# An attention and expert kernel on one core: the attention phase written anew, with every turning done by transposing DMAs

## The chip, the cores and the metric

One core of one Trainium2 chip runs the whole kernel. The metric is the device time of one execution in microseconds (us); lower is better. Below, PE is TensorE, PEld its weight loads, DVE is VectorE, ACT is ScalarE, POOL is GpSimd and SP is SyncE, whose queue issues the DMAs that no other engine issues. PSUM is the memory of eight banks (128 partitions x 2 KB each) into which PE writes.

## The reference

32 batches of 128 tokens with 512 numbers each pass through one attention layer and one mixture-of-experts layer:

```python
x = x + xattn(layernorm(x), mask, ctx)          # 32 heads of 16 numbers
x = x + moe(layernorm(x))                       # 8 experts, the best 2 for each token

def xattn(h, mask, ctx):
    q, k, v = h @ Wq, h @ Wk, h @ Wv            # split into 32 heads
    q, k = rope(q), rope(k)
    w = softmax(q @ k.T / 4 + mask)             # over the batch's own 128 keys
    out = w @ v
    a_k, a_v = ctx @ Wk, ctx @ Wv               # 128 more keys, no rope, no mask
    out += tanh(gate) * softmax(q @ a_k.T / 4) @ a_v
    return out @ Wo

def moe(h):                                     # 2 of 8 experts by router logits
    gate, up = split(h @ w1[e]); y = (silu(gate) * up) @ w2[e]
```

There are thus two softmaxes for each head and batch: the "own" path (path 0, masked) and the "adapter" path (path 1).

## The kernel before

The kernel has two phases, each a block in which every engine has its own program; engines meet only at semaphores. The attention phase goes through the 32 batches and writes the residual sum, the normalized rows for the experts (`h_pairs`) and eight lists of tokens. The expert phase then works through 71 tiles of 128 listed rows; it isn't touched by the change.

Matmuls of f32 accuracy are made of f16 halves: a value is split into a high part and what is left (`xcs`, `ohs`, `qs`, `ks`, `aks` hold both), and `project` sums three terms of four chunks each, 12 matmuls of 512 columns. There are six large projections for each batch: `q`, `k`, `ak`, `v`, `avp`, `out_project`.

PE contracts over partitions, so what it contracts must be turned. Before the change PE turns it, by matmuls with an identity, and ACT copies the result out of PSUM:
- `x_turn`, `out_turn`, `h_turn` (helper `transposes`, L1075): 8 tiles of 128x128 each for the normalized input, the attention's output and the normalized rows of the router, and three ACT copies (`x_turned`, `out_T`, `h_transposed`; L530, L598, L609).
- `stack` (helper `turn_pairs`, L1120): q, k and adapter k of two heads at a time, 48 tiles for each batch, into the banks `ma`, and eight ACT copies `stack_out` (L570) into `qkk`. `qkk` is a ring of five slots; a slot holds one octet of heads (8 heads: 4 pairs of 2 rows of 64 partitions).

The scores are computed twice. First directly, queries on the partitions, to get each query's maximum: `half_scores` (L1145) writes 4 heads of one path to one of the two banks `md`, DVE adds the mask (L795, path 0 only) and takes the maxima (`maxima`, L799, one call a bank). PE turns the maxima (`max_turn`, L1156). Then turned, keys on the partitions, which the product with the values wants: `scores_T` writes to the two banks `st` first the turned mask as two f32 matmuls of 512 columns for each bank (L1172), then adds the scores (L1178) and the negative maxima (L1183). ACT takes the exponential bank by bank (`exps`, L576), PE multiplies with the values (`values`, L1197) into the banks `av`, and the sums go back through ACT (`values_T`, L582) and PE (`values_back`, L1205).

Every engine's order is written out by hand. The function `step(b, c, d, n, m)` of each engine is called once a batch: b is the batch whose turned scores are under way, n the next, m the one after it, d and c the two before. Each engine works strictly in the order of its `step`, so a wait holds back all that stands behind it. The code outside the loop, `first` and `last`, fills and empties this order.

SP issues seven plain loads and stores in a batch's step, among them `wst` (a slice of the expert weights, which ACT and POOL split while attention runs).

## Time and profile before

| | |
|---|---|
| time, median of 3 runs | 1954.81 us (1952.67 to 1966.75) |
| profiled execution, span | 1957.9 us |
| PE busy | 1802.3 us, 92% |
| DVE busy | 1245.6 us, 64% |
| ACT busy | 1075.1 us, 55% |
| POOL busy | 751.8 us, 38% |
| DMA queue of SP | 65.96 MB, 10.3% of 16 engines' span |

The span runs from the first to the last instruction of one profiled execution. An engine is busy while an instruction runs on it; matmuls overlap one another, so their durations add up to more than the time that PE takes for them, and the time of a kind is better read from start to start. The page also shows the span in 40 slices, with the busy share of each engine in tenths.

### The profile page before, as it was taken

What the parts mean: (1) busy time and instruction counts of PE and PEld (TensorE: products, weight loads), DVE (VectorE), ACT (ScalarE), POOL (GpSimd) and SP (SyncE); (2) the same over time, 40 slices, a digit from 0 to 9 for tenths busy, and PEclk for the clock granted to TensorE, in tenths of its full rate; (3) what the DMA queues carried; (4) which work ended last, traced back from release to release, by engine and by line L of the source; (5) the groups of instructions that cost most, each with busy time, mean ns of one, the idle gap of its engine ahead of it and who ended that gap; (6) DMA issues with size and microseconds to landing.
All of it is one profiled execution on the core that took longest, in us unless ns stands there. A gap on an engine that the chain in (4) does not pass through costs nothing. (4 is left out here: it accounts for less than half of the span.)

```text
span 1957.9 us, 53291 instructions
## 1 busy us (share of the span) xinstructions
PE 1802.3 (92%) x19721; PEld 1094.1 (56%) x19722; DVE 1245.6 (64%) x3365; ACT 1075.1 (55%) x1716; POOL 751.8 (38%) x926
## 2 busy tenths in 40 slices
PE   3899899999999999999999999999845999999997
PEld 1555455555555555555555556555523666666664
DVE  4578677777788877778887777888644323332332
ACT  3465556666666666666666666666524444344432
POOL 3233433433333334433333443333223444444443
PEclk8899999999999999999999999999977999999999
DMA  3011111111111111111111111110014444444443
GB/s 135 26 37 37 37 38 37 38 43 43 62 38 38 37 37 43 44 62 38 38 37 38 43 50 55 38 38 32 29 63 112 82 85 85 80 82 86 84 79 63
DMA packets 64021, 106.00 MB, mean 54 GB/s; under 512 B 19088, under 2 KB 23184, under 8 KB 63312
## 3 DMA queue, kind: packets, MB, share of 16 engines
q0 software_dynamic: 18144, 37.31, 10.8%
q1 hardware_dynamic: 45680, 65.96, 10.3%
q8 instruction: 137, 2.24, 0.5%
q14 instruction: 60, 0.49, 0.1%
HBM read 67.51 MB, written 35.72 MB: 53 GB/s over the span
## 5 line engine op out<-in xcount | busy, mean ns | idle before, releaser
L576 ACT ACTIVATE pr<-st 128x512 f32<-128x512 f32 x512 | 285.5, 601 | 267.2 <-PE st L1183 248.3
L799 DVE TENSOR_REDUCE mx<-md 128x4 f32<-128x512 f32 x512 | 340.7, 688 | 20.8 <-PE md L1145 7.2
L1566 PE MATMUL y<-w1s,hgT 128*128 x1704 | 279.9, 315 | 3.6 <-ACT hgT L1480 3.6
L570 ACT ACTIVATE qkk<-ma 128x768 f16<-128x768 f16 x256 | 205.8, 817 | 84.2 <-PE ma L1120 84.2
L450 POOL TENSOR_TENSOR part<-part,tg_r 128x128 f32<-128x128 f32 x128 | 51.4, 402 | 474.8 <-DVE part L832 474.8
L1566 PEld LDWEIGHTS y<-w1s,hgT 128*128 128x128 f16 x1704 | 164.3, 98 | 95.5 <-issue 4.0
L1145 PE MATMUL md<-qkk 64*128 64x128 f16 x2048 | 166.8, 219 | 48.1 <-DVE mx L799 42.5
L795 DVE TENSOR_TENSOR md<-md,msk 128x512 f32<-128x512 f32 x256 | 177.1, 692 | 50.4 <-PE md L1145 50.4
L1197 PE MATMUL av<-pr,vv 128*17 128x128 f32 x4096 | 176.6, 277 | 2.8 <-ACT pr L576 2.1
L1145 PEld LDWEIGHTS md<-qkk 64*128 64x128 f16 x2048 | 100.6, 94 | 111.8 <-issue 85.6
L1480 ACT ACTIVATE hgT<-px 128x1024 f16<-128x1024 f16 x71 | 72.6, 1023 | 156.6 <-PE px L1556 156.6
L1172 PE MATMUL st<-identr,mskp 128*128 128x512 f32 x512 | 156.1, 426 | 1.3 <-DVE mT L822 0.8
L1585 PE MATMUL y<-w2s,yT 128*128 (+1 forms) x639 | 150.3, 379 | 0.9 <-DVE yT L1544 0.9
L1543 DVE COPY yT<-py 128x256 f16<-128x256 f16 x142 | 40.3, 284 | 148.2 <-PE py L1575 148.2
L760 DVE SCALAR_TENSOR_TENSOR aks<-ma,aks 128x512 f16<-128x512 f32 x64 | 41.2, 686 | 126.0 <-ACT aks L536 126.0
L1459 POOL DMA_INDIRECT out<-yo,dst x71 | 113.1, 1593 | 16.7 <-issue 12.1
L1197 PEld LDWEIGHTS av<-pr,vv 128*17 128x17 f32 x4096 | 81.4, 96 | 63.9 <-issue 32.7
L582 ACT ACTIVATE avT<-av 128x512 f32<-128x512 f32 x128 | 77.4, 604 | 56.8 <-PE av L1197 56.8
L407 POOL TENSOR_TENSOR t<-t 128x512 f32<-128x512 f32 x32 | 50.4, 1576 | 148.3 <-DVE t L773 148.3
L1172 PEld LDWEIGHTS st<-identr,mskp 128*128 128x128 f32 x512 | 88.8, 188 | 33.1 <-issue 6.9
L1178 PE MATMUL st<-qkk 64*128 64x128 f16 x2048 | 101.8, 219 | 0.2
L1183 PE MATMUL st<-mT,hsel 64*128 64x128 bf16 x2048 | 99.1, 216 | 0.0
(206 smaller groups left out, 3578.3 us busy)
## 6 DMA issues: line engine op xcount, KB each, us to landing
wst<-in_w SPq DMA_DIRECT2D x32, 352.0 KB, 3.1
cin<-in_ctx SPq DMA_DIRECT2D x32, 256.0 KB, 3.9
xin<-in_x SPq DMA_DIRECT2D x32, 256.0 KB, 3.5
xres<-in_x SPq DMA_DIRECT2D x32, 256.0 KB, 3.9
out<-x SPq DMA_DIRECT2D x32, 256.0 KB, 2.1
h_pairs<-ohs SPq DMA_DIRECT2D x32, 256.0 KB, 2.0
msk<-in_mask SPq DMA_DIRECT2D x32, 64.0 KB, 3.6
lrow<-lists SPq DMA_DIRECT2D x71, 1.0 KB, 3.5
```

The costliest lines, as they stand in the source:

```text
L570: act.activation(qkk[:, slot, :, j:j + 2, :], turned, ACT.Copy).then_inc(stk_o.sem, 1)
L576: act.activation(pr[:, r, :, :], st[r][:, :, :], ACT.Exp).then_inc(p_ex.sem, 1)
L795: dve.tensor_tensor(sm[r][:, :, :], sm[r][:, :, :], msk[:, n.par, :].unsqueeze(1).to_broadcast([P, 4, P]), ALU.add).then_inc(s_mask.sem, 1)
L799: dve.tensor_reduce(mx[:, 2 * path + r, 4 * o:4 * o + 4], sm[r][:, :, :], AX.X, ALU.max).then_inc(s_max[r].sem, 1)
L1145: i = pe.matmul(sm[r][:, j, :], qkk[rows, slot, 0, j, :], qkk[rows, slot, 1 + path, j, :], start=True, stop=True)
L1172: pe.matmul(st[r][:, :, :], mskp[:, n.par, part, :], identr[:, :].unsqueeze(1).to_broadcast([P, 4, P]), start=(part == 0), stop=False, ski ...
L1178: pe.matmul(st[r][:, j, :], qkk[rows, slot, 1 + path, j, :], qkk[rows, slot, 0, j, :], start=(path == 1 and j == 0), stop=False, skip_grou ...
L1183: i = pe.matmul(st[r][:, j, :], hsel[rows, p:p + 1].to_broadcast([64, P]), mT[rows, path, :], start=False, stop=(j == 3), skip_group_check ...
L1197: i = pe.matmul(av[o % 2][VC * j:VC * j + VW, 2 * path + r, :], vv[:, n.par, path, 8 * o + 2 * j + r, :], pr[:, r, j, :], start=True, stop ...
L1459: pool.indirect_dma_start(out=dram["out_rows"], out_offset=bass.IndirectOffsetOnAxis(ap=dst[:, s.off % LB:s.off % LB + 1], axis=0), in_=yo ...
L1566: i = pe.matmul(y1[s.par][j][:, 0:F], hgT[:, s.par, a, c, :], w, start=(n == 0), stop=(n == 11))
L1585: i = pe.matmul(y2[s.par][:, :], yT[0:fn, a, k, :], w, start=(n == 0), stop=(n == 8))
```

## The change

The expert phase stays. In the attention phase:
- All turning but that of the maxima and of the values' sums moves to transposing DMAs of SP: three of 128x1024 f16 (256 KB) for x, output and router rows, and twelve of 128x512 f16 (128 KB) for q, k and adapter k by octet, in each batch. `x_turn`, `out_turn`, `h_turn`, `stack` and the ACT copies behind them go.
- The mask comes twice, plain and turned (`mask_T`, turned on the host). ACT writes it into the banks before the scores are added: `seed_direct` into both banks `md`, `seed_turned` into both banks `st`, 1024 columns each, once an octet. The mask matmuls of PE (L1172) and the mask additions of DVE (L795) go, and so do the splits of the mask (L546, L712).
- The two banks `st` become one tensor, and so do the two `md`. `exps` and `maxima` take both banks with one instruction (1024 columns). `direct` alternates between the two halves of partitions, so that two small matmuls of different rows stand side by side.
- `ctx_lo` and `out_low` move from DVE to POOL.
- `xres` has one buffer and not two; the normalized rows have their own tile `hn`; `mT` gets a second buffer.
- Every engine gets a new order. `step(i)` runs each task for batch i minus a constant of its own; there is no `first` or `last`. `latest` puts one wait before a PE task that takes a bank which other groups have used. SP's order holds 15 transposing and 8 plain DMAs in each step.

The diff, cut to its core:

```diff
-    st = [ps(f"st{k}", [P, 4, P], F32) for k in range(2)]
+    st = ps("st", [P, 2, 4, P], F32)
     ma = [ps(f"ma{k}", [P, 512], F32) for k in range(2)]
-    md = [ps(f"md{k}", [P, 512], F32) for k in range(2)]
+    md = ps("md", [P, 2, 4, P], F32)
+    home = dict(q=1, k=0, ak=0, v=1, avp=0, o=1, router=0, places=1, mturn=1)
...
     @block.sync
+        def turn_x(n):
+            sp.wait_ge(x_lo.sem, x_lo.at(n))
+            for used in (q_p, k_p, v_p):
+                sp.wait_ge(used.sem, used.at(n.shift(-1)))
+            sp.dma_start_transpose(turned(xT), rows(xcs)).then_inc(x_T.sem, 16)
...
+        def turn_octet(n, o, plane, src, split, done):
+            slot, past, octet = place_of(n, o)
+            sp.wait_ge(split.sem, split.at(n))
+            sp.wait_ge(t_pe.sem, t_pe.at(past, 4 * octet + 4))
+            sp.dma_start_transpose(qkk[:, slot, plane, :, :],
+                                   src[:, 8 * o:8 * o + 8, :, :].rearrange("p h a d -> p (h a d)")
+                                   ).then_inc(done[o].sem, 16)
...
+        def step(i):
+            run(turn_q, i - 13, 2)
+            run(turn_k, i - 13, 2)
+            run(turn_ak, i - 13, 2)
+            run(turn_out, i - 15)
+            run(next_m_turned, i - 13)
+            run(next_w, i - 14)
+            run(turn_k, i - 13, 3)
+            run(load_residual, i - 15)
+            run(next_m, i - 12)
+            run(turn_q, i - 13, 3)
+            run(turn_ak, i - 13, 3)
+            run(store_out, i - 16)
+            run(turn_q, i - 12, 0)
+            run(next_x, i - 10)
+            run(turn_k, i - 12, 0)
+            run(turn_ak, i - 12, 0)
+            run(turn_q, i - 12, 1)
+            run(turn_x, i - 11)
+            run(next_c, i - 11)
+            run(turn_k, i - 12, 1)
+            run(turn_h, i - 15)
+            run(turn_ak, i - 12, 1)
+            run(store_h, i - 15)
...
     @block.scalar
-            act.activation(mskp[:, n.par, 0, :], msk[:, n.par, :], ACT.Copy).then_inc(m_hi.sem, 1)
+        def seed_direct(n, o):
+            act.wait_ge(d_max.sem, d_max.at(n, 2 * o))
+            act.activation(md[:, :, :, :].rearrange("p r j n -> p (r j) n"),
+                           msk[:, n.par, :].unsqueeze(1).to_broadcast([P, 8, P]), ACT.Copy).then_inc(d_seed.sem, 1)
+        def seed_turned(n, o):
+            act.wait_ge(p_ex.sem, p_ex.at(n, 2 * o))
+            act.activation(st[:, :, :, :].rearrange("p r j n -> p (r j) n"),
+                           mskT[:, n.par, :].unsqueeze(1).to_broadcast([P, 8, P]), ACT.Copy).then_inc(t_seed.sem, 1)
-        def stack_out(n, g):
-            act.activation(qkk[:, slot, :, j:j + 2, :], turned, ACT.Copy).then_inc(stk_o.sem, 1)
-        def exps(n, u):
-            r = u % 2
-            act.wait_ge(t_pe.sem, t_pe.at(n, u + 1))
-            act.wait_ge(av_pe.sem, av_pe.at(n, u - 1))
-            act.activation(pr[:, r, :, :], st[r][:, :, :], ACT.Exp).then_inc(p_ex.sem, 1)
+        def exps(n, w):
+            act.wait_ge(t_pe.sem, t_pe.at(n, 2 * w + 2))
+            act.wait_ge(av_pe.sem, av_pe.at(n, w))
+            act.activation(pr[:, :, :, :], st[:, :, :, :], ACT.Exp).then_inc(p_ex.sem, 1)
...
     @block.vector
-                if path == 0:
-                    dve.tensor_tensor(sm[r][:, :, :], sm[r][:, :, :],
-                                      msk[:, n.par, :].unsqueeze(1).to_broadcast([P, 4, P]),
-                                      ALU.add).then_inc(s_mask.sem, 1)
-                dve.tensor_reduce(mx[:, 2 * path + r, 4 * o:4 * o + 4], sm[r][:, :, :], AX.X,
-                                  ALU.max).then_inc(s_max[r].sem, 1)
+        def maxima(n, o, path):
+            dve.wait_ge(d_pe.sem, d_pe.at(n, 2 * (2 * o + path) + 2))
+            dve.tensor_reduce(mx[:, 2 * path:2 * path + 2, 4 * o:4 * o + 4], md[:, :, :, :], AX.X,
+                              ALU.max).then_inc(d_max.sem, 1)
...
     @block.tensor
+        def direct(n, o, path):
+            if path == 0:
+                pe.wait_ge(d_seed.sem, d_seed.at(n, o + 1))
+                pe.wait_ge(q_T[o].sem, q_T[o].at(n))
+                pe.wait_ge(k_T[o].sem, k_T[o].at(n))
+            else:
+                pe.wait_ge(d_max.sem, d_max.at(n, 2 * o + 1))
+                pe.wait_ge(ak_T[o].sem, ak_T[o].at(n))
             for j in range(4):
-                i = pe.matmul(sm[r][:, j, :], qkk[rows, slot, 0, j, :], qkk[rows, slot, 1 + path, j, :],
-                              start=True, stop=True)
-            i.then_inc(s_pe[r].sem, 1)
+                for r in range(2):
+                    rows = slice(64 * r, 64 * r + 64)
+                    i = pe.matmul(md[:, r, j, :], qkk[rows, slot, 0, j, :], qkk[rows, slot, 1 + path, j, :],
+                                  start=(path == 1 and j == 0), stop=(j == 3), skip_group_check=True)
+                    if j == 3:
+                        i.then_inc(d_pe.sem, 1)
...
-            if path == 0:
-                for r in range(2):
-                    for part in range(2):
-                        pe.matmul(st[r][:, :, :], mskp[:, n.par, part, :],
-                                  identr[:, :].unsqueeze(1).to_broadcast([P, 4, P]), start=(part == 0), stop=False,
-                                  skip_group_check=True)
```

## Rows read from the trace of the kernel before

**Rows 1.** The page: busy time, and the busy tenths in 40 slices.
```profile
PE 1802.3 (92%) x19721; PEld 1094.1 (56%) x19722; DVE 1245.6 (64%) x3365; ACT 1075.1 (55%) x1716; POOL 751.8 (38%) x926
...
PE   3899899999999999999999999999845999999997
```

**Rows 2.** Windows to the first L1156, to the last, to the first gather, the rest.
```profile
core 0: us, PE busy (x) PEld busy (x) DVE busy (x) ACT busy (x) POOL busy (x), PEclk, DMA share, GB/s
0.00:69.40 69.40, 36.53 (x199) 18.87 (x201) 35.32 (x60) 24.86 (x30) 14.70 (x35) 0.80 0.26 96
69.40:1408.10 1338.70, 1284.60 (x15810) 773.32 (x15809) 1030.39 (x2606) 835.72 (x1352) 505.69 (x586) 0.99 0.13 41
1408.10:1479.00 70.90, 28.84 (x377) 16.50 (x375) 35.29 (x123) 25.63 (x42) 16.33 (x23) 0.73 0.21 67
1479.00:1957.90 478.90, 452.31 (x3337) 285.45 (x3337) 144.61 (x577) 188.87 (x293) 215.08 (x283) 0.97 0.47 83
```

**Rows 3.** The window of one batch, from one turning of the maxima to the next.
```profile
722.33:765.02 42.69, 41.33 (x514) 24.98 (x514) 33.57 (x87) 27.18 (x44) 16.32 (x19) 1.00 0.13 43
```

**Rows 4.** Groups of that batch, PE (busy, mean ns, idle before, releaser).
```profile
L1145 PE MATMUL md<-qkk 64*128 64x128 f16 x64 | 5.1, 217 | 1.4 <-DVE mx L799 1.2
```

**Rows 5.** Timeline of PE within that batch (start, length, line, operation).
```profile
736.85 1.21 PE L1172 MATMUL st<-identr,mskp 128*128 128x512 f32 x4
737.99 0.40 PE L1178 MATMUL st<-qkk 64*128 64x128 f16 x8
738.22 0.39 PE L1183 MATMUL st<-mT,hsel 64*128 64x128 bf16 x8
738.57 0.28 PE L1120 MATMUL ma<-ident,qs 128*128 128x128 f16 x2
...
739.25 0.61 PE L1205 MATMUL av<-identr,avT 128*128 128x128 f32 x4
...
744.65 0.43 PE L1145 MATMUL md<-qkk 64*128 64x128 f16 x8
...
761.17 0.83 PE L1145 MATMUL md<-qkk 64*128 64x128 f16 x8
```

**Rows 6.** Groups of that batch, DVE.
```profile
L799 DVE TENSOR_REDUCE mx<-md 128x4 f32<-128x512 f32 x16 | 10.6, 688 | 0.6 <-PE md L1145 0.2
L795 DVE TENSOR_TENSOR md<-md,msk 128x512 f32<-128x512 f32 x8 | 5.5, 693 | 1.4 <-PE md L1145 1.4
L832 DVE TENSOR_TENSOR part<-av,rc 128x256 f32<-128x256 f32 x4 | 1.7, 424 | 0.1
```

**Rows 7.** Groups of that batch, ACT.
```profile
L576 ACT ACTIVATE pr<-st 128x512 f32<-128x512 f32 x16 | 8.9, 602 | 8.2 <-PE st L1183 7.9 <-PE av L1197 0.3
L570 ACT ACTIVATE qkk<-ma 128x768 f16<-128x768 f16 x8 | 6.4, 818 | 2.4 <-PE ma L1120 2.4
...
L551 ACT ACTIVATE qs<-t 128x1024 f16<-128x1024 f32 x1 | 1.0, 1048 | 0.0
L536 ACT ACTIVATE aks<-ma 128x1024 f16<-128x1024 f32 x1 | 1.0, 1024 | 0.0
```

**Rows 8.** Groups of that batch, POOL.
```profile
L402 POOL TENSOR_TENSOR xcs<-nat,xcs 128x512 f16<-128x512 f32 x1 | 1.2, 1156 | 3.8 <-ACT xcs L509 3.8
```

**Rows 9.** Timeline of SP's queue in that batch: a DMA's issue.
```profile
741.02 0.33 SPq L315 DMA_DIRECT2D h_pairs<-ohs  x1
...
745.85 0.43 SPq L285 DMA_DIRECT2D xin<-in_x  x1
```

**Rows 10.** The page: SP's DMA queue, and DMA issues with us to landing.
```profile
q1 hardware_dynamic: 45680, 65.96, 10.3%
...
wst<-in_w SPq DMA_DIRECT2D x32, 352.0 KB, 3.1
cin<-in_ctx SPq DMA_DIRECT2D x32, 256.0 KB, 3.9
...
h_pairs<-ohs SPq DMA_DIRECT2D x32, 256.0 KB, 2.0
```

More of the change, by code:

```diff
@@ L244, in whole, with run, walk, latest @@
         return isinstance(n.n, int) and n.n == 0
-    def walk(eng, step, first, last):
-        def near(b, lacks):
-            step(b, *(None if d in lacks else b.shift(d) for d in (-2, -1, 1, 2)))
-        first(Batch(0, 0))
-        for n in range(NB):
-            b = Batch(0, n)
-            near(b, [d for d in (-2, -1, 1, 2) if not 0 <= n + d < NB])
-        last(Batch(0, NB - 1))
+    def run(task, n, *args):
+        if 0 <= n < NB:
+            task(Batch(0, n), *args)
+    def walk(step):
+        for i in range(NB + 16):
+            step(i)
+    def latest(eng, n, *users):
+        for event, shift in users:
+            if 0 <= n.n + shift < NB:
+                eng.wait_ge(event.sem, event.at(n.shift(shift)))
+                return
     def place_of(n, o):
@@ new lines, in turn_q, with turn_k, turn_ak, load_first_w2 @@
+        def turn_q(n, o):
+            turn_octet(n, o, 0, qs, q_lo, q_T)
+        def turn_k(n, o):
+            turn_octet(n, o, 1, ks, k_lo, k_T)
+        def turn_ak(n, o):
+            turn_octet(n, o, 2, aks, ak_lo, ak_T)
+        def load_first_w2(n):
+            for used in (q_p, k_p, ak_p, v_p, av_p):
+                sp.wait_ge(used.sem, used.at(n))
+            for e in range(len(keep["w2f"])):
+                sp.dma_start(keep["w2f"][e][:, 0:2, :], dram["w2a"][e]).then_inc(keep["w2_in"][e], 16)
+                sp.dma_start(keep["w2f"][e][0:96, 2, :], dram["w2b"][e]).then_inc(keep["w2_in"][e], 16)
@@ L554, in k_high @@
             act.wait_ge(k_r.sem, k_r.at(n))
[L555 removed]
+            for turned in k_T:
+                act.wait_ge(turned.sem, turned.at(n.shift(-1)))
             act.activation(ks[:, :, 0:4:2, :], twice(t3), ACT.Copy).then_inc(k_hi.sem, 1)
@@ L1065, in experts_slots, with step @@
             assert made[0] == TAB
-        walk(dve, step, first, last)
+        def step(i):
+            run(residual, i - 5)
+            run(maxima, i - 3, 3, 1)
+            run(neg_max, i - 3)
+            run(turned_max, i - 3)
+            run(stats_h, i - 5)
+            run(ak_low, i - 2)
+            run(norm_h, i - 5)
+            run(normal, i - 4, 2)
+            run(h_low, i - 5)
+            run(maxima, i - 2, 0, 0)
+            run(stats_x, i)
+            run(normal, i - 4, 3)
+            run(router_weights, i - 6)
+            run(maxima, i - 2, 0, 1)
+            run(router_counts, i - 6)
+            run(normal, i - 3, 0)
+            run(maxima, i - 2, 1, 0)
+            run(norm_x, i)
+            run(rotate_q, i - 1)
+            run(maxima, i - 2, 1, 1)
+            run(router_rows, i - 6)
+            run(rotate_k, i - 1)
+            run(maxima, i - 2, 2, 0)
+            run(normal, i - 3, 1)
+            run(router_logits, i - 5)
+            run(maxima, i - 2, 2, 1)
+            run(router_top, i - 5)
+            run(maxima, i - 2, 3, 0)
+        walk(step)
+        experts_slots()
     @block.tensor
     def _(pe):
-        def transposes(bank, src):
-            for part in range(2):
-                for c in range(NC_):
-                    i = pe.transpose(half(bank)[:, part * NC_ + c, :], src[:, part, c * P:(c + 1) * P], ident16[:, :])
-            return i
         def project(bank, xt, w, cols=D):
@@ new lines, in _, with step @@
+        pe.wait_ge(dve_c.sem, 2)
+        for bank in (st[:, 0, :, :], st[:, 1, :, :], md[:, 0, :, :], md[:, 1, :, :]):
+            i = pe.matmul(bank, ident_bf[:, :], ident_bf[:, :].unsqueeze(1).to_broadcast([P, 4, P]),
+                          start=True, stop=True)
+        i.then_inc(banks_open.sem, 1)
+        def step(i):
+            run(scores_T, i - 6, 4)
+            run(k, i - 4)
+            run(scores_T, i - 6, 5)
+            run(values, i - 6, 4)
+            run(direct, i - 5, 2, 0)
+            run(values_back, i - 6, 1)
+            run(router, i - 8)
+            run(values, i - 6, 5)
+            run(direct, i - 5, 2, 1)
+            run(scores_T, i - 6, 6)
+            run(out_project, i - 7)
+            run(direct, i - 5, 3, 0)
+            run(scores_T, i - 6, 7)
+            run(values, i - 6, 6)
+            run(values_back, i - 6, 2)
+            run(direct, i - 5, 3, 1)
+            run(ak, i - 4)
+            run(max_turn, i - 5)
+            run(values, i - 6, 7)
+            run(scores_T, i - 5, 0)
+            run(v, i - 4)
+            run(values_back, i - 6, 3)
+            run(scores_T, i - 5, 1)
+            run(direct, i - 4, 0, 0)
+            run(values, i - 5, 0)
+            run(avp, i - 4)
+            run(values, i - 5, 1)
+            run(direct, i - 4, 0, 1)
+            run(scores_T, i - 5, 2)
+            run(places, i - 8)
+            run(values_back, i - 5, 0)
+            run(values, i - 5, 2)
+            run(scores_T, i - 5, 3)
+            run(direct, i - 4, 1, 0)
+            run(q, i - 3)
+            run(values, i - 5, 3)
+            run(direct, i - 4, 1, 1)
```

805 lines of the change are left out of this document (266 added, 539 removed).

## The prediction

> **What bounds the kernel now.** I read the page first, for the shares by engine and by slice. PE is busy for 92% of the span and in nearly every slice of the first 28, while DVE, ACT and POOL are busy for 64%, 55% and 38% [rows 1]. The windows then cut the span in four [rows 2]: 69.4 us until the first batch's maxima are turned, 1338.7 us from there to the same instruction of the last batch, 70.9 us of emptying up to the first gather, and 478.9 us of experts. The second stretch holds 31 steps of one batch, so a step takes 1338.7 / 31 = 43.18 us. That number is what the change can move; the experts aren't touched. In one step of 42.69 us PE is busy for 41.33, DVE for 33.57, ACT for 27.18 and POOL for 16.32 [rows 3]. PE sets the step: it stands still for some 1.4 us only, nearly all of it before L1145, waiting until DVE has read the banks `md` [rows 4]. So each us of PE work taken out of a step is worth 31 us, until another engine, a chain through the banks, or SP's queue takes over.
>
> **The change part by part, PE first.** Durations of matmuls overlap, so I take starts.
> - Mask matmuls: four from 736.85 to 737.99, 1.14 us, and four such groups a batch: 4.6 us go [rows 5].
> - Turning q, k and adapter k: twelve tiles from 738.57 to 739.25, 0.68 us or 57 ns each; 48 tiles are 2.7 us, with the gaps to the next work about 2.9 us. The 24 tiles of `transposes` at the same 57 ns are 1.4 us. Together 4.3 us go [rows 5].
> - Direct scores: the eleven merged rows of L1145 in this batch (first and last in [rows 5]), each counted from its start to the start of the next row, come to 5.9 us for 64 matmuls, stalls included. Side by side they become what the turned scores are already: eight of L1178 from 737.99 to 738.22, 0.23 us [rows 5]. 64 of those take 1.9 us, so 4.0 us go if the stalls go with them. The stalls are DVE's, and DVE becomes faster (below).
> - Values, projections, the negative maxima and the sums' way back stay as they are.
>
> PE's work in a step is then 42.7 - 4.6 - 4.3 - 4.0 = 29.8 us. This is the floor of the step, a gain of 13.4 us on 43.18.
>
> **DVE.** The mask additions go, 5.5 us [rows 6]. Sixteen reductions of 512 columns at 0.688 us become eight of 1024. No row has that form; 256 columns take 0.424 and 512 take 0.69 us, which is 1.04 ns a column [rows 6], so 1024 take about 1.22 us, and 11.0 becomes 9.8 us. `ctx_lo` and `out_low`, of 512 columns too, leave with some 0.7 us each, and the mask split with a quarter of that size, 0.3 us. DVE has 33.6 - 5.5 - 1.2 - 1.7 = 25.2 us of work.
>
> **ACT.** Eight copies to `qkk` at 0.818, three of 1024 columns at 1.02 and the mask's high part at 0.3 go: 9.9 us. Sixteen exponentials at 0.602 (9.6 us) become eight of 1024 columns; the nearest rows of that size are 1.02 from PSUM and 1.05 from SBUF [rows 7], so 8.2 us. Eight seeds at 1.05 come, 8.4 us; no row writes 1024 f32 columns to PSUM, and I take the reading rows for both ends. ACT has 27.2 - 9.9 - 1.4 + 8.4 = 24.3 us. The seeding thus costs ACT nearly what the copies give back, and it is free only because ACT isn't the bound: were it the bound, it would cost 8.4 x 31 = 260 us.
>
> **POOL** takes two subtractions of 512 columns, 1.16 us each [rows 8]: 16.3 + 2.3 = 18.6 us.
>
> **The chains through the banks.** A bank pair is now used as a whole and has no second copy. For `st` an octet runs: seed 1.05, scores and negative maxima about 0.6, exponential 1.02, scores 0.6, exponential 1.02; 4.3 us, with five hand-overs of some 0.1 to 0.15 us about 4.9, four octets 20 us. For `md`: seed 1.05, then twice scores of about 0.4 and a reduction of 1.22, again 4.9 and 20 us. Both are under 29.8. The ring of five slots closes a third chain: octet 3 of the next batch can be turned only once octet 2 of this one has been used in `scores_T`; its direct scores, maxima, the turning of the maxima (with DVE's five small steps, an estimated 2.5 us) and two thirds of the next `st` chain (15 us) stand behind that. With three transposing DMAs of 3 to 4 us from issue to landing I get 24 to 26 us a step. So the chains are 4 to 10 us shorter than the floor of PE, which must cover all queueing behind other tasks. In the kernel before, the same kind of hand-written order loses 1.4 of 42.7 us.
>
> **SP's queue, the unknown.** Fifteen transposing DMAs come in each step; no row of this trace is one. Behind each stand, in order, the other turnings and all loads, and behind these PE. What the rows say: a plain issue holds the queue for 0.33 to 0.43 us [rows 9], so eight plain ones are 3.0 us, and fifteen more at 0.4 would be 6. That is the lower bound, 9 us of a step. From issue to landing a plain 256 KB takes 2.0 us as a store and up to 3.9 us as a load [rows 10]. If each transposing DMA held the queue until it landed, a step would be 15x + 3.0 us with x between 2.0 and 3.9: 33 to 61.5 us, the upper bound. In bandwidth, 12 x 128 KB + 3 x 256 KB is 2.4 MB; the queue's present 65.96 MB took 10.3% of 1957.9 us, 327 GB/s [rows 10], at which they are 7 us on the sixteen engines. I take a holding time under 1.8 us, where the queue isn't the bound (15 x 1.79 + 3.0 = 29.8), since the nearest rows in kind, the issues of the same queue, are a quarter of that; the landing rows stay as the upper end.
>
> On this the Trainium skill speaks both ways, and no row here can decide. "Advanced Engine Details and Errata", section "X-Bar Transpose (TRN2)", has transposing DMAs as fast as plain ones. Against the change speaks a table in "DMA: Bandwidth & Descriptors", section "Why a DMA increments its semaphore by 16 and not by 1": on generations before the newest, the issuing engine spends 262,144 cycles on 8,192 tiles turned from SBUF to SBUF, 32 cycles a tile. It names no tile size; if a tile were 2 KB, 128 KB would hold SP for 2,048 cycles, and at the 1.2 GHz of "TensorE: Matmul & The Clock Gate" a step would be an estimated 18 x 1.7 + 3.0 = 34 us.
>
> **The sum.** To the 29.8 us I add 1.5 us for waits that remain (the kernel before has 1.4) and 0.5 us because the mean step before (43.18) was that much longer than the one that I took apart. The step is 31.8 us, and the 31 steps give 31 x (43.18 - 31.8) = 353 us. Filling and emptying, 69.4 and 70.9 us, stay about as they are: PE has slack there, and each turning on the way of the first and the last batch trades an ACT copy of 1 us behind PE for a DMA of 2 to 4 us; I add 5 us. 1957.9 - 353 + 5 = 1610 us. The median of the runs lies 3 us under the profiled execution, so 1607 us.
>
> **The rivals.**
> 1. The chains, not PE. The `md` and `st` chains share ACT, whose work is 24 of 30 us, and DVE, with 25 of 30; a seed that is late behind another ACT task delays scores, maxima and the ring. For it: no bank has a partner any more, and each loop needs three engines. Against: 4 to 10 us of slack. It gives steps of 34 to 37 us, taking 35.5: 1957.9 - 31 x 7.7 + 5 - 3 = 1721 us. In the trace ACT and DVE would wait for each other around `md` and `st`, with PE under 90%.
> 2. SP's queue is the bound, but below the old step. A holding time between 1.8 and 2.68 us (15x + 3.0 between 30 and 43.2) does it; near 2.3 us the step is 37.5 us, 1957.9 - 31 x 5.7 + 5 - 3 = 1783 us. For it: 23 issues in order, each with waits of its own, and the store's landing of 2.0 us [rows 10] falls in this band. Against: plain issues don't hold the queue until they land. The skill's rule of 32 cycles a tile belongs here, and with a tile of 2 KB it ends near 1670 us.
> 3. The other side: the same mechanism with the price of a load. Once a transposing DMA keeps the queue for more than 2.68 us, the step passes 43.2 us and the kernel is slower. At the 3.1 us of the fastest load row [rows 10] the step is 49.5 us and the time 1957.9 + 31 x 6.3 + 5 - 3 = 2155 us. PE would then stand still for many us at a stretch, and its clock, 0.99 of full in the steady stretch and 0.73 to 0.80 where PE waits a lot [rows 2], would fall too.
> 4. That the floor is lower than I think (the direct scores cost nothing beside others, or the waits vanish): 29.5 us and no waits is 1957.9 - 31 x 13.7 = 1533 us, the low end.
>
> **How the numbers follow.** A measurement of this kernel can tell about 1% from no change, 20 us. The forecast (PE bound, steps of 30 to 33.5 us, 1550 to 1660 us) has 0.58, with what lies under it. Rival 1 has 0.13, rival 2 has 0.15, rival 3 has 0.12, and 0.02 is left for a time near the old one. All but rival 3 and that rest are faster: 0.86 faster, 0.02 the same, 0.12 slower. The range goes from 1535, the floor, to 1800, which takes in rival 1 and most of rival 2 and leaves rival 3 and the rest of rival 2 out.
>
> **What would show it.** In the new profile: a PE step of 30 to 33 us between two turnings of the maxima; PE busy over 90% in it; eight reductions near 1.22 us and sixteen ACT instructions near 1.0 us for seeds and exponentials; DVE about 25, ACT about 24 and POOL about 19 us a step. SP's issues of transposing DMAs in the timeline show the holding time at once: under 1.8 us I am right on the queue, above it rivals 2 and 3 follow with their sums. What makes me wrong most is that holding time, then waits of PE for `q_T`, `k_T`, `d_seed` or `t_seed`.

## The result, and the profile after

The changed kernel takes 1854.84 us, the median of 4 runs (1844.53 to 1861.64), beside 1956.3 us for the kernel before on the same chip: 0.9452 of its time, 95% interval 0.9405 to 0.95. It is 5.5% faster. The prediction said 1607 us and 18%, and its range ended at 1800. The profiled execution has a span of 1842.8 us. Its page, with the busy shares, PE's tenths and granted clock in 40 slices, SP's DMA queue and the largest groups, answers to [rows 1, 6, 7, 10]:

```profile
PE 1506.1 (82%) x16909; PEld 864.2 (47%) x16910; DVE 1111.3 (60%) x2755; ACT 1023.0 (56%) x1332; POOL 835.0 (45%) x991
...
PE   4788777888888787788878888887519999999996
...
PEclk9999899998999999989999899999659999999999
...
q1 hardware_dynamic: 360560, 143.61, 40.6%
...
L787 DVE TENSOR_REDUCE mx<-md 128x8 f32<-128x1024 f32 x256 | 313.0, 1222 | 238.4 <-PE md L1071 235.4
L646 ACT ACTIVATE pr<-st 128x1024 f32<-128x1024 f32 x256 | 260.9, 1019 | 167.8 <-PE av L1116 135.6
...
L623 ACT ACTIVATE st<-mskT 128x1024 f32<-128x1024 f32 x128 | 131.8, 1030 | 5.6
```

PE lost 296 us of work, as planned, but its slices in the attention phase read 7 and 8 where they read 9 [rows 1]. No engine is full any more. The windows cut where [rows 2] cut say how much is idle:

```profile
0.00:68.00 68.00, 32.12 (x164) 12.79 (x165) 37.62 (x51) 22.89 (x25) 30.16 (x44) 0.90 0.47 132
68.00:1286.50 1218.50, 993.86 (x13060) 549.52 (x13064) 887.77 (x1987) 786.54 (x981) 563.30 (x631) 0.95 0.57 104
1286.50:1364.00 77.50, 27.12 (x360) 16.06 (x348) 40.93 (x143) 24.67 (x34) 27.27 (x36) 0.60 0.36 105
```

The 31 steps take 1218.5 us, 39.3 us each, where 31.8 was forecast. PE is busy for 993.9 / 31 = 32.1 us of a step (29.8 forecast) and idle for 7.2 us (1.5 forecast, and 0.5 for the mean step). DVE is busy for 28.6 us of a step, where 25.2 was forecast; ACT (25.4) and POOL (18.2) lie within 1.1 us of their forecasts. Everything outside these steps takes 624.3 us, 5.1 us more than before; the forecast added 5 for it. So the whole miss lies in the step. The view of waits for the same stretch (total us, times, longest) names what PE waits for, and what holds ACT:

```profile
ACT ohs L663 <- DMA h_pairs<-ohs: 96.1, 29, 4.4
...
PE av L1116 <- ACT pr L646: 71.9, 62, 3.3
...
PE ma L1080 <- DVE mp L805: 53.4, 27, 2.8
PE md L1071 <- DMA qkk<-qs: 44.0, 19, 3.7
...
PE md L1071 <- issue: 27.2, 12, 4.8
...
PE md L1071 <- DMA qkk<-ks: 14.3, 18, 1.7
```

Four things hold PE, none for more than 72 us: the exponentials (2.3 us a step), the split maxima `mp` (1.7), the turned q and k of an octet (1.9), and 0.9 for which the profile names no releaser. How they come about is seen in one step, from one turning of the maxima (705.37) to the next (746.06). First SP's queue, in the timeline (start, length; the length is the time that the DMA holds the queue):

```profile
730.29 1.20 SPq L347 DMA_TRANSPOSE qkk<-ks  x1
731.53 0.58 SPq L288 DMA_DIRECT2D xres<-in_x  x1
732.15 2.43 SPq L298 DMA_DIRECT2D msk<-in_mask  x1
734.68 1.20 SPq L347 DMA_TRANSPOSE qkk<-qs  x1
```

This step is the slowest of its kind: 2.43 us is the longest that the mask's load holds the queue, and its median over the stretch is 0.43 us. An ordinary step has k and q 2.4 us apart and not 4.4:

```profile
528.48 1.20 SPq L347 DMA_TRANSPOSE qkk<-ks  x1
...
530.34 0.43 SPq L298 DMA_DIRECT2D msk<-in_mask  x1
530.87 1.80 SPq L347 DMA_TRANSPOSE qkk<-qs  x1
```

Then PE, its timeline in the first of these steps (in brackets: idle before, and the releaser):

```profile
723.67 0.63 PE L1116 MATMUL av<-pr,vv 128*17 128x128 f32 x16 [2.62 <-ACT pr L646]
...
725.70 3.93 PE L1017 MATMUL ma<-w_k,xT 128*128 128x512 f16 x12
...
733.56 2.76 PE L1017 MATMUL ma<-w_o,oT 128*128 128x512 f16 x12
738.50 0.40 PE L1071 MATMUL md<-qkk 64*128 64x128 f16 x8 [2.18 <-DMA qkk<-qs]
...
746.06 0.28 PE L1080 MATMUL ma<-ident_bf,mp 128*128 128x128 bf16 x2 [2.53 <-DVE mp L805]
```

The last scores that use the ring slot, L1101 at 729.80, end near 730.2. SP turns k of octet 3 at once, then loads the residual and the mask, and turns q only at 734.68: 4.4 us after the slot was free, and 2.4 us in the ordinary step. q lands before 738.5, the direct scores of octet 3 follow, their maxima, DVE's split, and the next turning. This is the ring chain of the prediction, 24 to 26 us there; it closes the loop here at some 40 us. It isn't a chain of bare durations: 25 us of it, from 705.4 to 730.2, is PE's own order of other tasks and its wait for `pr`.

The split shows something that no part of the prediction had. In the timeline of all engines some us earlier, DVE's two small steps on 64 columns (L796, L798) take 1.99 and 1.11 us; the same forms took a mean of 194 and 225 ns in the kernel before:

```profile
701.27 2.13 POOL L500 TENSOR_TENSOR ks<-t,ks 128x1024 f16<-128x1024 f32 x1 [0.16 <-ACT ks L636]
701.46 1.99 DVE L796 TENSOR_SCALAR mp<-mx 128x64 bf16<-128x64 f32 x1
...
703.36 1.16 POOL L477 TENSOR_TENSOR xcs<-nat,xcs 128x512 f16<-128x512 f32 x1
...
703.49 1.11 DVE L798 SCALAR_TENSOR_TENSOR mr<-mx,mp 128x64 f32<-128x64 f32 x1
...
704.63 0.19 DVE L801 CAST mp<-mr 128x64 bf16<-128x64 f32 x1
```

L796 ends at 703.45, and POOL's L500 at 703.40; L798 ends at 704.60, and POOL's L477 at 704.52. The small steps end when POOL's large instruction ends. From 68 to 1230 us 54 DVE instructions on 8 or 64 columns take more than 0.6 us, and all 54 end within 0.12 us of the end of a POOL instruction of over 1 us. It isn't all of DVE that is held: a `MAX8` on 8 columns lies wholly beside such a POOL instruction 27 times and is never stretched. The two steps are stretched in most batches, as their means over the stretch say (busy, mean ns), here of the changed kernel:

```profile
L796 DVE TENSOR_SCALAR mp<-mx 128x64 bf16<-128x64 f32 x31 | 41.0, 1321 | 1.1
L798 DVE SCALAR_TENSOR_TENSOR mr<-mx,mp 128x64 f32<-128x64 f32 x31 | 31.7, 1023 | 1.1
```

and of the kernel before, where the same form isn't stretched:

```profile
L809 DVE TENSOR_SCALAR mp<-mx 128x64 bf16<-128x64 f32 x28 | 5.4, 194 | 2.6
```

### The profile page after: what moved, and what is told of

Its sections match the earlier page's. It is cut to its first block and busy times, and to the rows that moved or that the text cites. A ratio compares the mean times of both kernels' runs of the same rounds, so it can differ in the third digit from the quotient of the medians.

```text
span 1842.8 us, 46904 instructions
## 1 busy us (share of the span) xinstructions
PE 1506.1 (82%) x16909; PEld 864.2 (47%) x16910; DVE 1111.3 (60%) x2755; ACT 1023.0 (56%) x1332; POOL 835.0 (45%) x991
## 3 DMA queue, kind: packets, MB, share of 16 engines
q1 hardware_dynamic: 360560, 143.61, 40.6%
## 5 line engine op out<-in xcount | busy, mean ns | idle before, releaser
L787 DVE TENSOR_REDUCE mx<-md 128x8 f32<-128x1024 f32 x256 | 313.0, 1222 | 238.4 <-PE md L1071 235.4
L646 ACT ACTIVATE pr<-st 128x1024 f32<-128x1024 f32 x256 | 260.9, 1019 | 167.8 <-PE av L1116 135.6
L1071 PE MATMUL md<-qkk 64*128 64x128 f16 x2048 | 106.6, 226 | 104.5 <-DMA qkk<-qs 44.0
L615 ACT ACTIVATE md<-msk 128x1024 f32<-128x1024 f32 x128 | 130.9, 1022 | 20.8 <-DVE mx L787 20.0
L1071 PEld LDWEIGHTS md<-qkk 64*128 64x128 f16 x2048 | 63.7, 97 | 159.0 <-issue 138.1
L623 ACT ACTIVATE st<-mskT 128x1024 f32<-128x1024 f32 x128 | 131.8, 1030 | 5.6
L504 POOL TENSOR_TENSOR ohs<-on,ohs 128x512 f16<-128x512 f32 x32 | 37.0, 1155 | 212.3 <-ACT ohs L663 212.3
L491 POOL TENSOR_TENSOR qs<-t,qs 128x1024 f16<-128x1024 f32 x32 | 70.6, 2205 | 127.4 <-ACT qs L630 127.4
L1101 PE MATMUL st<-mT,hsel 64*128 64x128 bf16 x2048 | 107.6, 228 | 0.0
L1017 PE MATMUL ma<-w_k,xT 128*128 128x512 f16 x384 | 101.7, 421 | 0.0
L1017 PE MATMUL ma<-w_k,cT 128*128 128x512 f16 x384 | 98.5, 411 | 1.7 <-issue 1.7
```

Source lines behind the costliest of these rows:

```text
L615: act.activation(md[:, :, :, :].rearrange("p r j n -> p (r j) n"), msk[:, n.par, :].unsqueeze(1).to_broadcast([P, 8, P]), ACT.Copy).then_i ...
L623: act.activation(st[:, :, :, :].rearrange("p r j n -> p (r j) n"), mskT[:, n.par, :].unsqueeze(1).to_broadcast([P, 8, P]), ACT.Copy).then_ ...
L646: act.activation(pr[:, :, :, :], st[:, :, :, :], ACT.Exp).then_inc(p_ex.sem, 1)
L787: dve.tensor_reduce(mx[:, 2 * path:2 * path + 2, 4 * o:4 * o + 4], md[:, :, :, :], AX.X, ALU.max).then_inc(d_max.sem, 1)
L1017: i = pe.matmul(bank[:, 0:cols], xt[:, a, c, :], w[:, c, z, :], start=(n == 0), stop=(n == 11))
L1071: i = pe.matmul(md[:, r, j, :], qkk[rows, slot, 0, j, :], qkk[rows, slot, 1 + path, j, :], start=(path == 1 and j == 0), stop=(j == 3), sk ...
```

## The experiments

Four theories follow from this. A: buffers without a partner. `ohs` serves first the output's halves and then the router rows, so `out_hi` (L663) waits for the store of `h_pairs`, the last of three DMAs in SP's order, and ACT's exponentials wait behind it; and five ring slots with q late in SP's order make the ring chain the step (the expectations below call this part the ring theory). B: DVE's small steps on SBUF stand still while a POOL instruction runs. C: the DMA engines' throughput, 57% busy in the steady stretch, makes every landing late. D: the chains through the banks `md` and `st` are full, as in rival 1 of the prediction. All kernels are taken against the kernel before on their own chip. A difference between two of them is given as the difference of the two ratios, times 1960 us; from the two intervals together it is sure to some 10 to 14 us either way.

**1. The control.** A new tile needs room, so the normalized x is written in place and `nat` goes. The next load into that buffer then waits until both halves of x are made, where it waited for the normalization only. Cut to its core:

```diff
-            dve.tensor_scalar(nat[:, :], xin[:, n.par, :], ...)
+            dve.tensor_scalar(xin[:, n.par, :], xin[:, n.par, :], ...)
-            act.activation(xcs[:, 0, :], nat[:, :], ACT.Copy)
+            act.activation(xcs[:, 0, :], xin[:, n.par, :], ACT.Copy)
```

> Control. The changed kernel with the normalized input written over the loaded input, so that the tile nat goes and 2 KB of each partition come free for the runs after it. Every theory expects the time of the changed kernel, 1855 us, give or take 15 us. A larger gain would mean that the wait of the normalization for the halves of the batch before was itself on the path.

Measured: 1867.13 us, 0.9491 (0.9447 to 0.9535). Its interval overlaps that of the changed kernel, 8 us apart; it stands as the control for 2 and 5.

**2. The output's halves in a tile of their own**, on top of the control (cut):

```diff
+    oos = sb("oos", [P, 2, D], F16)
-            act.wait_ge(h_T.sem, h_T.at(n.shift(-1)))
-            act.wait_ge(h2_st.sem(n.shift(-1)), h2_st.at(n.shift(-1)))
-            act.activation(ohs[:, 0, :], on[:, :], ACT.Copy)
+            act.wait_ge(o_T.sem, o_T.at(n.shift(-1)))
+            act.activation(oos[:, 0, :], on[:, :], ACT.Copy)
```

> As the in-place control, but the attention's output is split into a tile of its own and no longer into the tile that also holds the router rows and is stored as h_pairs. Theory A (single buffers that are handed over through SP's queue hold PE back): ACT's 96 us of waiting at L663 for the h_pairs store go, and with them most of PE's 72 us before L1116, so 40 to 70 us less, 1785 to 1815 us. Theory B (DVE stretched by POOL's long instructions) and theory D (the chains through the banks md and st are full): the wait moves elsewhere, less than 15 us change.

Measured: 1814.93 us, 0.9243 (0.9188 to 0.9297), 49 us under the control. ACT's wait at L663 for the store is gone. The waits, 68 to 1286 us, say what became of PE's:

```profile
PE md L1070 <- DMA qkk<-qs: 79.9, 19, 8.9
...
PE av L1115 <- ACT pr L647: 21.0, 38, 1.2
```

PE's wait for `pr` falls from 65.5 us in the control to 21.0, but its wait for the turned q rises from 61.8 to 79.9: part of what one wait gives back seems to go to the next. The single buffer is shown as a cause, worth about 1.6 us of a step.

**3. POOL's long instructions cut**, in the changed kernel: the low halves of q and of k (2.1 us each) and of x (1.16 us) in four pieces each.

```diff
-            pool.tensor_tensor(qs[:, :, 2:4, :], twice(t1), qs[:, :, 0:2, :], ALU.subtract).then_inc(q_lo.sem, 1)
+            for h in range(0, NH, 8):
+                i = pool.tensor_tensor(qs[:, h:h + 8, 2:4, :], twice(t1)[:, h:h + 8], qs[:, h:h + 8, 0:2, :],
+                                       ALU.subtract)
+            i.then_inc(q_lo.sem, 1)
```

> The changed kernel with POOL's instructions of 2.1 us (low halves of q and k) in four pieces each and that of 1.16 us (low half of x) in four. Theory B: DVE's first two instructions of the maxima's split, 1.32 and 1.02 us in the mean where the kernel before has 0.19 and 0.23, end when a POOL instruction ends; with short ones they fall below 0.7 us, PE's 53 us of waiting at L1080 halve, and the time falls by 25 to 50 us. Theory A: the same time within 10 us.

Measured: 1851.08 us, 0.9404 (0.9349 to 0.946), not told apart from the changed kernel. The mechanism moved and the time didn't. The groups, same stretch:

```profile
L806 DVE SCALAR_TENSOR_TENSOR mr<-mx,mp 128x64 f32<-128x64 f32 x31 | 18.9, 610 | 1.1
L804 DVE TENSOR_SCALAR mp<-mx 128x64 bf16<-128x64 f32 x31 | 16.5, 533 | 1.1
```

They fell from 1.32 and 1.02 us to 0.53 and 0.61, and PE's wait at the turning from 53.4 to 40.4 us. But PE's waits before the direct scores, for q, for k and without a releaser, grew from 85.5 to 97.8 us over the same stretch. That the time came back there fits, but isn't shown by these two profiles: they are the slowest execution of this kernel and the fastest of the changed one, 17 us apart. A miss, for my expectation took the wait as its own price.

**4. No turning of the adapter's k.** The ring's adapter plane holds zeros and is never written, so the adapter's scores are left out; four of fifteen turnings and the waits of PE and ACT for them go (cut).

```diff
-            run(turn_ak, i - 13, 2)
...
-                pe.wait_ge(ak_T[o].sem, ak_T[o].at(n))
+        const(pool.memset(qkk[:, :, 2, :, :], 0.0))
```

> The changed kernel without its four transposing DMAs of the adapter keys in each step: that plane of qkk is filled with zeros once at the start, so the adapter scores are left out of the result while every matmul, exponential and maximum stays. SP's queue loses 4 x 1.2 us of a step. Theory A: PE's waits for the turned q and k (some 85 us with those put down to issue) shrink, 1770 to 1820 us. Theory C (the DMA engines themselves, 57% busy, make landings late): the same size, and the landings of q and k fall from 3.4 and 2.8 us towards 2.4. Theory D: no change beyond 15 us.

Measured: 1826.61 us, 0.9286 (0.9242 to 0.933), 33 us less, just above the range of A. The landings stay: q from 3.4 to 3.7 us, k from 2.8 to 2.9, though q1's share falls from 40.6% to 37.2%. C asked for shorter ones, and isn't borne out. SP has more time, and spends it on the ring (the waits of SP, same stretch; 155.5 us in the changed kernel):

```profile
SPq L346 <- PE st L1095: 365.4, 76, 8.6
```

**5. Six ring slots**, on top of the control: `RING = 5` becomes `RING = 6`.

> The in-place control with six slots in the ring qkk and not five. Ring theory (the step is the length of the loop octet 2 used in scores_T, slot free, octet 3 of the next batch turned, landed, scored directly, maxima, turning of the maxima, scores_T again; in the changed kernel that loop takes some 40 us, 24 from the turning of the maxima to the fifth scores_T and 16 from there to the next turning): a slot more lets octet 3 be turned two calls of scores_T, some 8 us, earlier, so the SP queue's waits for scores_T (155 us) fall to under a third and the time falls by at least 60 us against the control, to 1800 us or less. Theory D (bank chains) and theory B (DVE stretched): within 20 us of the control.

Measured: 1798.89 us, 0.9183 (0.9138 to 0.9228), 60 us under the control. SP doesn't wait for the scores any more; its longest waits are now for the halves of q. PE's wait for the turned q falls from 58.9 us to 27.8 (68 to 1230 us). The ring chain was a bound: 1.9 us of a step.

**6. q first in SP's order**, five slots: q, k and adapter k of octet 3 stand together, before the residual's and the mask's load.

```diff
+            run(turn_q, i - 13, 3)
             run(turn_k, i - 13, 3)
+            run(turn_ak, i - 13, 3)
             run(load_residual, i - 15)
             run(next_m, i - 12)
-            run(turn_q, i - 13, 3)
-            run(turn_ak, i - 13, 3)
```

> The changed kernel with one thing moved in SP's order: the turning of q for octet 3 stands before that of k, and the loads of the residual and of the mask stand behind the three turnings of octet 3 and no longer between them. In the changed kernel the turning of q is issued 4.4 us after the slot is free (at 734.7, slot free near 730.3); moved, it is issued some 3 us earlier. Ring theory: the whole 2 to 3 us come off each step, 60 to 90 us, 1765 to 1795 us. Theories B and D: no change beyond 15 us. Theory C (transfers limited by the DMA engines): the landing moves less than the issue, under 30 us gain.

Measured: 1826.82 us, 0.9326 (0.9283 to 0.9368), 25 us less, where I expected 60 to 90. PE's wait for q is gone from the list and one for k stands in its place, 61.4 us in 41 times of 68 to 1230, with 38.6 us for DVE's maxima behind it, which the changed kernel doesn't have. Theory C said under 30 us too, but for another reason, that the landing moves less than the issue. The traces show that the issue itself moved less than I thought. I had read 4.4 us from the slowest step. Over all steps the median from the start of the first to the end of the second of the two turnings falls from 3.6 us to 2.5, since no load stands between them any more; 1.1 us in 31 steps is an estimated 34 us. The median landing of q falls from 3.4 us to 2.5, and that of k rises from 2.8 to 3.0.

**7. No turning of octets at all.** The whole ring holds zeros, so all scores are left out; twelve turnings and all waits for them go, and with them the ring chain and 50 MB of transfers.

> The changed kernel without its twelve transposing DMAs of q, k and adapter k in each step; qkk is filled with zeros once, so scores are left out of the result while all matmuls, maxima, exponentials and seeds stay, with the waits for the turned octets gone. x, output and router rows are still turned by DMA. It shows the step without the ring. Ring theory: PE is the bound at 31 to 33.5 us a step, 1590 to 1670 us. Theory D: the seeds, exponentials, maxima and banks hold the step above 36 us, over 1750 us.

Measured: 1774.07 us, 0.9048 (0.9014 to 0.9082). The ring theory said 1590 to 1670; it fell as the whole story, and the number is the one that D named, over 1750. As things stand here, all that the octets' turning costs through ring, queue and engines is 79 us of a miss of 248. That isn't its upper limit: kernel 9 comes back to both points. PE now waits mostly in one place, before L1051, for DVE (the waits, 68 to 1230 us):

```profile
PE md L1051 <- DVE mx L770: 136.1, 27, 5.2
```

DVE's timeline before such a wait shows its small router steps, which do the choice of experts on 8 columns, usually some 0.2 us, at 2 us:

```profile
728.80 2.13 DVE L850 TENSOR_TENSOR key<-key,iota 128x8 f32<-128x8 f32 x1
...
731.17 0.16 DVE L856 TENSOR_REDUCE lowest<-key 128x1 f32<-128x8 f32 x1
731.37 1.86 DVE L859 TENSOR_SCALAR oh<-iota,lowest 128x8 f32<-128x8 f32 x1
733.27 1.07 DVE L863 TENSOR_TENSOR sel<-oh 128x8 bf16<-128x8 f32 x1
734.26 1.21 DVE L770 TENSOR_REDUCE mx<-md 128x8 f32<-128x1024 f32 x1
```

POOL's timeline has the ends that they share:

```profile
728.78 2.14 POOL L480 TENSOR_TENSOR qs<-t,qs 128x1024 f16<-128x1024 f32 x1 [1.10 <-ACT qs L615]
731.08 2.13 POOL L489 TENSOR_TENSOR ks<-t,ks 128x1024 f16<-128x1024 f32 x1 [0.16 <-ACT ks L619]
733.16 1.15 POOL L466 TENSOR_TENSOR xcs<-nat,xcs 128x512 f16<-128x512 f32 x1
```

The small reduction L856 is the exception again: 0.16 us at 731.17, wholly beside POOL's L489, and 27 times so in the stretch. And PE pays twice, for the wait and for the clock after it: its next projection takes 4.08 us where 2.76 is usual, at a granted clock of 0.67 of full, so in part at the lower of its two levels (1.2 and 2.4 GHz).

```profile
735.53 0.61 PE L1051 MATMUL md<-qkk 64*128 64x128 f16 x8 [5.19 <-DVE mx L770]
736.07 4.08 PE L1000 MATMUL ma<-w_k,cT 128*128 128x512 f16 x12
```

With the ring gone, DVE's order has slid against POOL's: the three long instructions now meet the router's steps, and not those of the maxima. A wait was cured and another took its place.

**8. All of A in one kernel that leaves nothing out**: the output's tile of its own, six slots, q first, and x in place in a single `xin` (for the room; the next load then waits for the halves of the x before it).

> Output halves in their own tile, six slots, the normalized input in place with one buffer for the loaded input, and SP's order with q first. If the gains stand beside one another (48 us of the tile, 60 of the slot, some of the order) it is 1700 to 1760 us. If ring and order cure the same wait, as the ring theory has it, the sum is less than its parts, 1740 to 1790 us. Theory D: 1800 us or more, as with the tile alone.

Measured: 1770.56 us, 0.9024 (0.8986 to 0.9063). That is the time of kernel 7, which has no octet turnings at all, but not for the same reasons (7 keeps the shared tile). Alone the three parts are worth 49, 60 and 25 us, 134 together; they give 84 against the changed kernel and 92 against the control. That fits parts that shorten the same loop, but no pair of them was run, and the single `xin` costs something of its own: SP waits 61.3 us for the halves of x. SP doesn't wait for the ring any more. PE's longest waits are (68 to 1230 us):

```profile
PE md L1070 <- DVE mx L786: 69.1, 22, 5.2
PE md L1070 <- DMA qkk<-ks: 46.7, 32, 5.1
```

**9. Kernels 7 and 3 together**: no octet turnings, and POOL's three cut.

> The run without octet turning (scores left out as there), with POOL's three instructions for the low halves of q, k and x in four pieces each. In that run DVE's small steps of the router (L850, L859, L863, mean 1.0, 1.0 and 0.95 us where the kernel before has 0.25, 0.23 and 0.17) end together with POOL's instructions of 2.1 us, hold back a reduction that PE waits for (136 us in 27 times before L1051), and the third direct score starts 5 us late. Theory B (DVE is held while POOL runs): those steps fall to 0.6 us or less, PE's wait falls by two thirds, and the step from 37.1 to 33 to 34.5 us, 1650 to 1700 us. If the wait for DVE is only the shape of DVE's order, the time stays within 20 us of 1774.

Measured: 1687.86 us, 0.8601 (0.8562 to 0.8641), 88 us less than kernel 7, by an edit that gives POOL nine more instructions a batch and takes no work away. The steps of the router fall to 0.38, 0.31 and 0.56 us, PE's wait by 58%, and the step from 37.1 to 34.3 us, nearly all as expected of B. The window of its steps, its wait for the maxima, and the mean of the router's step (1015 ns in kernel 7) are:

```profile
68.00:1130.00 1062.00, 957.27 (x13078) 535.10 (x13078) 867.66 (x1989) 779.94 (x982) 603.70 (x898) 0.96 0.31 74
```

```profile
PE md L1059 <- DVE mx L778: 57.3, 27, 2.2
```

```profile
L858 DVE TENSOR_TENSOR key<-key,iota 128x8 f32<-128x8 f32 x58 | 22.3, 384 | 2.0
```

B is shown for such steps: the same cut that gave nothing measurable in the changed kernel gives 88 us without the octets' turnings. D falls with it as the reason for kernel 7's time: seeds, exponentials, reductions and banks are all still there, and the step is 34.3 us, under the 36 that D set as a floor. And what the turnings cost depends on B in the same way. Without them the kernel is 79 us faster with POOL's instructions whole (the changed kernel and 7), and 157 us faster with them cut (3 and 9).

**10. Kernel 8 with POOL's three cut.**

> The combined kernel (output halves apart, six slots, q first) with the same short POOL instructions. Theory B with the ring theory: here too PE waits for DVE's reductions, 69 us, and gains 60 to 90 us, 1680 to 1715 us. If short instructions help nothing, as they did alone on the changed kernel (8 us, within its noise), 1760 to 1775 us.

Measured: 1736.64 us, 0.8867 (0.8811 to 0.8922), 31 us less than kernel 8. This is the fastest that computes all of the reference, 11.3% faster than the kernel before and 6% faster than the change. It is half of the least that I expected. PE's wait for DVE's maxima falls to 17.2 us (69.1 in kernel 8, both from 68 to 1230 us), and its waits, 68 to 1130 us, show k's landing in the lead:

```profile
PE md L1078 <- DMA qkk<-ks: 52.6, 31, 4.4
```

**11. All of POOL's instructions over 1 us cut**, on top of kernel 10: the low half of the context, the two rotations and the weights' low half too.

> As the run before, with all of POOL's instructions over 1 us in pieces (also the sums of q and k, the context's low half and the expert weights). Theory B: another 10 to 40 us, from the router's steps L927 and L859 of 1.36 and 0.88 us. Against: more pieces cost POOL some 3 us of a step, which it has.

Measured: 1775.7 us, 0.9045 (0.9 to 0.909), 35 us slower than kernel 10, where I expected 10 to 40 us less: a miss. DVE got faster still where it met them (the router's step on 16 columns, `chosen`, from 1452 ns to 388). But each of the two rotation sums takes POOL four times 0.46 us where it took 1.27 once, so q and k come out some 0.6 us later each, and PE's wait for k's landing doubles:

```profile
PE md L1085 <- DMA qkk<-ks: 103.1, 31, 5.9
```

Cutting has its own price. That it was the larger one here because the cut work is what the turning waits for fits the trace; the pieces weren't tried one by one.

## Why the prediction was wrong

The sign was right, and the size was off by three: 5.5% for 18%. Step by step:

- **The floor of PE: too low by 2.3 us, 71 us in 31 steps.** PE's work in a step is 32.1 us, for 29.8 forecast, and 30.9 in kernel 9. The mask matmuls and the turning went as planned. The direct scores side by side take 0.22 to 0.50 us for eight, from start to start (in the step shown 2.76 us for 64, not 1.9). Some 1.2 us of the step shown is the clock: the projection at 725.70 takes 3.93 us at a granted clock of 0.70, and the one at 733.56 takes 2.76 at 1.00. The slow one begins 2.0 us after the 2.62 us of waiting that end at 723.67, and the granted clock of the stretch is 0.95, for 0.99 before.
- **The new forms: right.** Reductions of 1024 columns take 1222 ns (1.22 forecast), exponentials 1019, seeds 1030 (1.02 to 1.05), and filling and emptying cost 5.1 us more (5).
- **The holding time of a transposing DMA: right**, and rivals 2 and 3 with it fell. It is 1.2 us in most and at most 3.0; fifteen hold the queue for 19.7 us of a step, and all its DMAs for 24.3, under the step of 39 us. A sixth slot gives 60 us without taking one DMA out: the queue's throughput isn't the bound; when each turning may start is.
- **Bandwidth: wrong by more than two, without consequence that a run shows.** I had 7 us of the sixteen engines a step. If the old traffic takes what it took, the 77.65 MB that came took 748 - 202 = 546 us of them (40.6% of 1842.8, less 10.3% of 1957.9), 142 GB/s for the 327 of plain traffic, 17 us a step.
- **What failed: the sum's term "1.5 us for waits that remain".** It is 7.2 us, 5.2 more than the sum had with its 0.5, of the 7.5 us that the step is too long; the other 2.3 are the floor's. I took it from the old order, in which PE was full and ACT could wait 8.2 us a step ahead of its exponentials at no cost [rows 7]; in a new order with PE at 82% of the steps the same term is set by the hand-overs. Two pieces make up most of it. First, the ring chain of "24 to 26 us" was a sum of durations; as a loop it also holds whatever PE and SP have queued ahead of each link, and with 2.4 us of SP's order (4.4 in the step shown) and 25 us of PE's it closes at the step's 39 to 40 us. "4 to 10 us of slack" was no slack: one more slot gave 60 us (run 5). Second, nothing in the sum had the single `ohs`, 49 us by run 2, or DVE's standing still beside POOL. The latter is worth 88 us by runs 7 and 9, 31 us by runs 8 and 10, and nothing that can be measured in the changed kernel as it is (run 3). It also is 1.9 of the 3.4 us that DVE is over its forecast in a step, by L796 and L798 alone.
- **Rival 1** had the right kind, chains in place of PE, with PE under 90% as it said, and 0.13 for its chance. It named the bank chains and ACT's late seeds. PE waits for a seed 2.8 us once in the stretch up to 1230 us. PE does wait 71.9 us for ACT's exponentials, which belong to the `st` chain and come late behind another ACT task, as the rival said of the seeds; but a second tile in SBUF alone takes two thirds of that away (run 2). So the chains that decide go through SBUF buffers and the ring, and the `md` chain shows first in kernels 6 to 10, as waits for DVE's maxima. Its 1721 us lies near the best that the repairs reach, 1737 us, which is a coincidence, and far from the change.

A rule of the Trainium skill bears on one part of the missing term, the held DVE steps, though it gives no size. "SBUF — State Buffer", section "SBUF: two separate sides", says that DVE and GpSimd share one pair of ports under an exclusive lock, held for the whole instruction, when a DVE instruction runs in a two-port mode, or has two SBUF inputs while the GpSimd instruction reads SBUF. The trace agrees where it can: L798, with two SBUF inputs, ends with POOL's instruction, which reads SBUF (0.23 us stretched to 1.11), while `MAX8` and the small reduction L856 of kernel 7, with one input, aren't stretched (0.17 and 0.16 us), and the large reduction, which reads PSUM, stays at 1222 ns beside the same POOL work. L796 is stretched too (0.19 to 1.99) with one tensor as input; the trace doesn't say which mode it runs in. On the turning, "Advanced Engine Details and Errata", section "X-Bar Transpose (TRN2)", has transposing DMAs as fast as regular ones; the 142 and 327 GB/s above say otherwise for pieces of this kind. The 32 cycles a tile that the prediction took from the Trainium skill don't appear as a price by size: 128 and 256 KB hold SP for 1.20 and 1.25 us, nearly alike.

Open is the rest between kernel 9, 1688 us, and the 1607 forecast. In its steps PE is idle for (1062 - 957.3) / 31 = 3.4 us, of which the maxima are 57.3 us in 31 steps, with the router's step still at 384 ns (251 before); which order would take that out wasn't tried. Against kernel 9 the best full kernel, 10, is 52 us slower, and k's landing leads PE's waits in it with 52.6 us; a cure for that wasn't run. Also open is which 27.2 us PE spends before L1071 with no releaser in the trace, and what hides B's gain in run 3, the ring alone or more: runs 7 and 9 show the gain with the ring and the transfers gone together, and runs 8 and 10 show 31 us of it with the ring's wait gone and the transfers in place.

## What to carry to other kernels

When a change takes the full engine off the bound, its old waiting time says nothing of the new one: walk each loop that a single buffer closes (bank pair, ring slot, shared tile), and count in it not only the durations but all that stands queued ahead of each link on each engine, the DMA queue too. When a step is read from one stretch of the timeline, look whether it is an ordinary one: 4.4 us in the step shown was 2.4 in most. Before moving work to POOL, look where its long instructions will lie beside DVE's small SBUF steps; cut them into pieces there, but not those that the next engine is waiting for. A wait's total doesn't say what curing it gives: here 134 us of single repairs gave 92 together, and one cure worth nothing measurable alone gave 88 us once another bound was gone.

## What the runs showed of the hardware

- Some small DVE steps on SBUF (0.17 to 0.23 us) take as long as the POOL instruction beside them still runs: 1.99 and 1.11 us for 64 columns, 2.13 and 1.86 for 8. They are `TENSOR_SCALAR`, `TENSOR_TENSOR` and `SCALAR_TENSOR_TENSOR`. `MAX8` (0.17 us), a reduction on SBUF (0.16) and the reductions out of PSUM (1.22) aren't touched.
- A transposing DMA from SBUF to SBUF holds SP's queue for 1.2 us, at 128 KB as at 256 KB, sometimes 2 to 3, beside 0.33 to 0.58 for most plain ones; in the changed kernel it lands 2.4 to 3.4 us after its issue (medians by tile).
- Transposing DMAs used the sixteen DMA engines at 142 GB/s, in packets under 512 bytes for the most part: q1 has 360560 packets, for 45680 before.
- Twelve matmuls of 512 columns take 2.76 us at a granted clock of 1.00, and 3.93 or 4.08 at 0.70 or 0.67, soon after PE has stood still for 2.6 or 5.2 us; in the emptying stretch, PE busy for a third of it, the granted clock was 0.60.
